# Two late slots of an expert network brought to their nodes by a matrix product instead of by memory

## The reference

```python
scores = x @ Wg + bg
topk_vals, topk_idx = jax.lax.top_k(scores, K)      # K = 2 of 8 experts
gates = jax.nn.softmax(topk_vals, axis=-1)
...
for e in range(NE):
    h = _gelu(x @ W1[e] + b1[e])
    h = _gelu(h @ W2[e] + b2[e])
    y = h @ W3[e] + b3[e]
    out = out + comb[..., e:e + 1] * y
```

## Time and profile before

| | us |
|---|---|
| median of three runs | 2332.95 |
| the runs | 2332.95, 10635.34, 2326.77 |
| the profiled execution, its own time | 2339.89 |
| its span in the profile | 2338.1 |
| network 0, first slot's output to last | 1233.8 to 1362.1 |
| network 1, first slot's output to last | 1981.7 to 2311.6 |

### The profile page before, as it was taken

How to read it: one execution, slowest core, us unless ns; L and a number is a source line. 1 busy time by engine, 2 the same in 40 slices (tenths; PEclk the granted TensorE clock), 3 DMA queues, 4 the chain that set the end, 5 groups by cost and what they waited for, 6 DMA issues and landing times. The chain is left out here.

```text
span 2338.1 us, 32237 instructions
## 1 busy us (share of the span) xinstructions
PE 2099.8 (90%) x12766; PEld 2018.1 (86%) x12766; DVE 1426.8 (61%) x2283; ACT 922.3 (39%) x1220; POOL 393.7 (17%) x216
## 2 busy tenths in 40 slices
PE   6998999999999999999869949788889968999994
PEld 5888999998999999999849949687789947999994
DVE  7645555555763233333459864358984777888884
ACT  2343155555341111111127723125522225777771
POOL 1672400000301434343010022210000020000001
PEclk9999999999999999999969979999999968999997
DMA  6212233333330211110159951110122047999995
GB/s 220 42 29 83 81 116 116 118 133 119 131 139 30 64 41 41 61 41 21 53 196 335 324 197 61 48 45 28 64 65 85 1 154 276 377 375 367 376 365 172
DMA packets 158240, 326.89 MB, mean 140 GB/s; under 512 B 14377, under 2 KB 99337, under 8 KB 158091
## 3 DMA queue, kind: packets, MB, share of 16 engines
q1 hardware_dynamic: 133354, 265.66, 32.5%
q10 hardware_dynamic: 18976, 43.31, 5.3%
q0 software_dynamic: 5760, 15.86, 2.2%
HBM read 278.22 MB, written 46.49 MB: 139 GB/s over the span
## 5 line engine op out<-in xcount | busy, mean ns | idle before, releaser
L656 PE MATMUL banks<-weight_hi,xt_hi 128*128 128x384 f32 (+2 forms) x2208 | 738.9, 335 | 45.3 <-DVE xt_lo L1432 14.3
L659 PE MATMUL banks<-weight_lo,xt_hi 128*128 128x384 f32 (+2 forms) x2208 | 723.5, 328 | 0.0
L660 PE MATMUL banks<-weight_hi,xt_lo 128*128 128x384 f32 (+2 forms) x2208 | 722.8, 327 | 0.0
L656 PEld LDWEIGHTS banks<-weight_hi,xt_hi 128*128 128x128 f32 x2208 | 423.3, 192 | 57.0 <-issue 28.2
L659 PEld LDWEIGHTS banks<-weight_lo,xt_hi 128*128 128x128 f32 x2208 | 423.4, 192 | 0.4 <-issue 0.2
L660 PEld LDWEIGHTS banks<-weight_hi,xt_lo 128*128 128x128 f32 x2208 | 422.5, 191 | 0.0
L1897 DVE TENSOR_TENSOR weight_lo<-weight_raw,weight_hi 128x2304 fp32r<-128x2304 f32 (+2 forms) x153 | 340.9, 2242 | 57.6 <-ACT weight_hi L1160 57.1
L1160 ACT ACTIVATE weight_hi<-weight_raw 128x2304 fp32r<-128x2304 f32 (+2 forms) x153 | 286.7, 1883 | 100.9 <-DMA weight_raw<-L_ffn_w_in 44.1
L859 POOL TENSOR_TENSOR weight_hi<-weight_raw,columns 128x2304 fp32r<-128x2304 f32 x20 | 80.6, 4029 | 700.3 <-DMA weight_raw<-L_gnn_root_in 322.6
L1660 DVE TENSOR_TENSOR held_lo<-banks,held_hi 128x384 fp32r<-128x384 f32 x80 | 44.6, 558 | 213.0 <-ACT held_hi L1087 213.0
L2517 PE MATMUL banks<-held_hi,a_rel 128*128 128x384 f32 (+1 forms) x550 | 170.6, 338 | 3.6 <-ACT a_rel L1102 2.8
(11 more groups left out here) (404 smaller groups left out, 3486.9 us busy)
## 6 DMA issues: line engine op xcount, KB each, us to landing
weight_raw<-L_ffn_w_in SPq DMA_DIRECT2D x102, 1152.0 KB, 7.7
weight_raw<-L_gnn_W_in SPq DMA_DIRECT2D x32, 1152.0 KB
weight_raw<-L_ffn_W_in SPq DMA_DIRECT2D x17, 1152.0 KB, 9.9
products<-bias_rows SPq DMA_DIRECT2D x80, 192.0 KB, 1.9
slot_in<-slot_rows ACTq DMA_DIRECT2D x34, 384.0 KB, 5.6
slot_out<-bias_rows ACTq DMA_DIRECT2D x34, 384.0 KB, 7.2
weight_raw<-L_ffn_W_in SPq DMA_DIRECT2D x17, 576.0 KB, 9.0
product_back<-products SPq DMA_DIRECT2D x10, 960.0 KB, 4.7
```

What stands on the lines that cost most here:

```text
L656: ins = pe.matmul(dst, s[0], m[0], start=start, stop=False)
L659: pe.matmul(dst, s[0], m[1], start=False, stop=False)
L660: return pe.matmul(dst, s[1], m[0], start=False, stop=stop)
```

## The change

The outputs of slots 15 and 16 (`LATE = 2`) no longer go to memory. Instead:

- `slot_out` ends at slot 14. POOL's ten gathers wait for the stores up to slot 14 only, and read row `min(place, 1919)`. They land in buffers that are free by then (the slot inputs, `y_rows`, and the two further raw buffers; from tile 2 on POOL also waits until the last weight unit has left those). The gate of a choice whose row lies in slot 15 or 16 is set to zero for them.
- ACT's queue writes the rows' numbers (before the first turn) and the gates (turn 3) to memory, 128 by 10 floats each, and at turn 5 reads them back broadcast to all partitions (two DMAs of 128 by 1280 floats).
- At turn 8 DVE runs `late_rows`: it finds for each row of slots 15 and 16 its gate, and builds a 0/1 matrix of each slot (128 rows by 640 nodes) in columns of `XT` that the network does not use.
- The outputs of slots 15 and 16 are multiplied by the rows' gates, split into high and low part (ACT, then DVE) and kept in `XT`. For each tile TensorE multiplies them with the 0/1 matrices (`late_products`, 8 matmuls), and DVE adds the result to `X` (`late_sums`).
- The sums with the gathered rows are moved ahead of the last slot's output on DVE: all five tiles in network 1, tiles 0 and 1 in network 0 (tile 2 follows that output; tiles 3 and 4 are added in the mixer's loop).
- The first Q unit's load is issued and its parts are split before the last slot's output; the second one's parts are split inside the mixer's loop.

Four semaphores of the routing are merged into others, which moves no work. The diff, without those:

```diff
@@ -84,6 +84,11 @@
...
+LATE = 2
+LATE_FROM = XSLOTS - LATE
+LATE_ROW = LATE_FROM * SLOT_ROWS
+PLACES = TILES * CHOSEN * P // 4
@@ -582,7 +592,21 @@
...
-        out_rows = [[V, XN1], [x[:, :, :].rearrange("p k c -> p (k c)").bitcast(F32).rearrange("p (t d) -> p t d", t=TILES) for x in XT]]
...
+        choice_all = [x[:, 0:4, 2 * P:2 * P + PLACES] for x in XT_place]
+        late_row, late_gate = first_at[:, 0:LATE], is_more[:, 0:LATE]
+        place_main = others[:, :, :].rearrange("p t e -> p (t e)")[:, 0:CHOICES].bitcast(I32)
...
+
+        def late_cols(s, t):
+
+            return XT[s][:, 4 + t // 3, free.start + t % 3 * P:free.start + (t % 3 + 1) * P]
+
+        out_rows = [x[:, :] for x in slot_in] + y_rows + [r[:, i * DIM:(i + 1) * DIM] for r in raw_more for i in range(3)]
+        LAST_RAW = [max(u for u in range(SPLITS[n]) if UNIT_AT[n][u][0] >= 2) for n in range(2)]
+        LAST_RAW0 = max(u for u in range(SPLITS[0]) if UNIT_AT[0][u][0] == 0)
+        LATE_BANKS = [[0, 4, 6, 4, 6], [0, 5, 3, 0, 5]]
@@ -830,10 +854,12 @@
...
-            sp.wait_ge(e_lo[0], RAWS + SPLITS[0])
+            sp.wait_ge(e_lo[0], RAWS + LAST_RAW0 + 1)
...
             with sp.Fori(0, 3) as i:
                 for c in range(2):
+                    if c == 1:
+                        sp.wait_ge(e_lo[0], RAWS + SPLITS[0])
                     load(Unit(U_MIX1 + c, i, 2), chunks(a["L1_mix_w_qkv"])[:, :, ds((2 * i + c) * WCOL, WCOL)])
@@ -923,20 +949,25 @@
...
                 for b in range(2):
-                    pool.wait_ge(y_out[n][b], 16 * len(range(b, XSLOTS, 2)))
+                    pool.wait_ge(y_out[n][b], 16 * len(range(b, LATE_FROM, 2)))
+                pool.wait_ge(placed, 3 * (n + 1))
                 for t in range(TILES):
+                    if t == 2:
+                        pool.wait_ge(e_lo[n], RAWS + LAST_RAW[n] + 1)
                     for k in range(CHOSEN):
                         j = t * CHOSEN + k
-                        pool.indirect_dma_start(out=out_rows[n][k][:, t, :], out_offset=None, in_=slot_out_dram[n],
-                                                in_offset=bass.IndirectOffsetOnAxis(ap=place[:, j:j + 1], axis=0)).then_inc(back[t], 16)
+                        pool.indirect_dma_start(out=out_rows[j], out_offset=None, in_=slot_out_dram[n],
+                                                in_offset=bass.IndirectOffsetOnAxis(ap=place_main[:, j:j + 1], axis=0)).then_inc(back[t], 16)
 
             after_phase(pool, 2)
             expert_rows(0)
@@ -1183,6 +1214,13 @@
...
+                    if v >= LATE_FROM:
+                        s = v - LATE_FROM
+                        act.wait_ge(late_hot, TILES * LATE * (n + 1))
+                        for c, (bank, _, width) in enumerate(full_cols(n, last)):
+                            act.wait_ge(y_full[n], 2 * v + c + 1)
+                            act.activation(late_y[s][0][:, c, :], ps[:, bank, 0:width], ACT.Copy, scale=late_gate[:, s:s + 1]).then_inc(late_hi, 1)
+                        return
                     act.wait_ge(y_used[n], 2 * (v + 1))
                     act.dma_start(slot_at(slot_out_dram[n], v), y_rows[v % 2]).then_inc(y_out[n][v % 2], 16)
 
@@ -1193,7 +1231,16 @@
...
+                act.wait_ge(placed, 3 * n + 2)
+                act.dma_start(choice_dram[0], place_f[:, :]).then_inc(choice_moved, 16)
                 for turn in turns(n):
+                    if turn == 3:
+                        act.wait_ge(comb_ready, 2 * (n + 1))
+                        act.dma_start(choice_dram[1], gate[:, :, :].rearrange("p t k -> p (t k)")).then_inc(choice_moved, 16)
+                    if turn == 5:
+                        act.wait_ge(choice_moved, 64 * n + 32)
+                        for into, src in zip(choice_all, choice_dram):
+                            act.dma_start(into, src.rearrange("p j -> (p j)").partition_broadcast(P).rearrange("p (c n) -> p c n", c=4)).then_inc(choice_moved, 16)
                     for l, v in visits(n, turn):
                         if l > 0:
                             transposed_hi(l, v)
@@ -1210,11 +1257,11 @@
...
+                    act.wait_ge(e_used[0], LAST_RAW0 + 1)
+                    unit_hi(U_MIX1)
+                    act.activation(warm[:, LN_IN1:LN_IN1 + 1], eps_col[:, :], ACT.Sqrt)
                 rows_out(XSLOTS - 1)
-                if n == 0:
-                    act.wait_ge(e_used[0], SPLITS[0])
-                    for c in range(2):
-                        unit_hi(U_MIX1 + c)
 
             experts(0, a["L0_ffn_Wg"], a["L0_ffn_bg"], a["L0_ffn_b3"], [a["L0_ffn_b1"], a["L0_ffn_b2"]])
             end_phase(act, "act", 3)
@@ -1908,11 +1957,43 @@
...
-                    if v >= 2:
+                    if 2 <= v < LATE_FROM:
...
                     for c, (bank, cols, width) in enumerate(full_cols(n, last)):
+                        if v >= LATE_FROM:
+                            s = v - LATE_FROM
+                            hi, lo = at(late_y[s], slice(None), c)
+                            vec.wait_ge(late_hi, 2 * (LATE * n + s) + c + 1)
+                            vec.scalar_tensor_tensor(lo, ps[:, bank, 0:width], late_gate[:, s:s + 1], f32(hi), ALU.mult, ALU.subtract).then_inc(y_used[n], 1)
+                            continue
                         vec.wait_ge(y_full[n], 2 * v + c + 1)
...
+                def late_rows():
+
+                    vec.wait_ge(masks, 2 + 4 * (n + 1))
+                    vec.tensor_scalar(place_main, place_f[:, :], float(LATE_ROW - 1), None, ALU.min).then_inc(placed, 1)
+                    vec.wait_ge(choice_moved, 64 * n + 32)
+                    flat = gate[:, :, :].rearrange("p t k -> p (t k)")
+                    order.step(vec.scalar_tensor_tensor(flat, place_f[:, :], float(LATE_ROW), flat, ALU.is_lt, ALU.mult))
+                    vec.wait_ge(choice_moved, 64 * (n + 1))
+                    at_all = choice_all[0].rearrange("p c (n t k) -> p t k c n", t=TILES, k=CHOSEN)
+                    for s in range(LATE):
+                        sums = late_gate[:, s:s + 1], total[:, s:s + 1]
+                        for i in range(2):
+                            one_slot = slice(2 * i, 2 * i + 2)
+                            order.step(vec.scalar_tensor_tensor(choice_kept, choice_all[0][:, one_slot], late_row[:, s:s + 1], choice_all[1][:, one_slot],
+                                                                ALU.is_equal, ALU.mult, accum_out=sums[i]))
+                            order.wait()
+                        order.step(vec.tensor_tensor(sums[0], sums[0], sums[1], ALU.add))
+                        order.wait()
+                    for s in range(LATE):
+                        into = [late_cols(s, t).rearrange("p (c n) -> p c n", c=4) for t in range(TILES)]
+                        for t in range(TILES):
+                            order.step(vec.tensor_scalar(into[t], at_all[:, t, 0], late_row[:, s:s + 1], None, ALU.is_equal))
+                        order.wait()
+                        for t in range(TILES):
+                            vec.scalar_tensor_tensor(into[t], at_all[:, t, 1], late_row[:, s:s + 1], f32(into[t]), ALU.is_equal, ALU.add).then_inc(late_hot, 1)
 
                 for _ in range(FIRST[n]):
                     low()
@@ -1921,6 +2002,8 @@
...
+                    if turn == 8:
+                        late_rows()
@@ -1936,23 +2019,28 @@
...
+                if n == 0:
+                    unit_lo(U_MIX1)
+                for t in range(TILES if n == 1 else 2):
+                    expert_sums(n, t)
                 output(XSLOTS - 1)
-
                 if n == 0:
-                    for c in range(2):
-                        unit_lo(U_MIX1 + c)
+                    expert_sums(0, 2)
...
 
                 rows = slice(0, LAST if t == FULL else P)
                 vec.wait_ge(back[t], 16 * CHOSEN * (n + 1))
                 for k in range(CHOSEN):
-                    ins = vec.scalar_tensor_tensor(X[rows, t, :], out_rows[n][k][rows, t, :], gate[rows, t, k:k + 1], X[rows, t, :], ALU.mult, ALU.add)
-                    if n == 0 or k == 0:
-                        order.step(ins)
-                        order.wait()
-                    else:
-                        ins.then_inc(rows_done, 1)
+                    order.step(vec.scalar_tensor_tensor(X[rows, t, :], out_rows[t * CHOSEN + k][rows, :], gate[rows, t, k:k + 1], X[rows, t, :], ALU.mult, ALU.add))
+                    order.wait()
+
+            def late_sums(n, t):
+
+                rows, bank = slice(0, LAST if t == FULL else P), LATE_BANKS[n][t]
+                x_row = X[rows, t, :].rearrange("p (c n) -> p c n", c=2)
+                vec.wait_ge(y_full[n], 2 * XSLOTS + t + 1)
+                vec.tensor_tensor(x_row, ps[rows, bank:bank + 2, 0:WCOL], x_row, ALU.add).then_inc(y_used[n], 1)
 
             experts(0)
             end_phase(vec, "vec", 3)
@@ -1962,7 +2050,12 @@
...
-                expert_sums(0, t)
```

(30 more changed lines are left out.)

55 lines of the change are left out of this document (34 added, 21 removed).

## The result

The changed kernel takes **2355.82 us** in the median of 4 runs (2348.79 to 2363.86) against 2332.55 for the kernel before, run beside it: 1.0106 [1.0083, 1.0130], 24.7 us more (one run of the kernel before at 10635 us is left out of the ratio). The forecast was 2334.5 and the range ended at 2348: **the prediction was wrong**, by 21 us, although the tail of network 1, at which the change aims, came out as forecast.

A forecast was written before the change was run, and what follows sets the result against it. Bounds: TensorE, DVE and memory near their limits in network 1, loads late in network 0, a serial 27.1 us tail. Terms -14.5 + 2 + 6 + 1 + 5 + 2 = +1.5 us, by the median 2334.5; range 2320 to 2348.

The forecast's parts named there:

- Tail of network 1, -14.5: End of network 1: late products and additions replace the serial gathers and sums after the last expert matmul, -14.5 us.
- I take full clock: Network 1's tail: TensorE's 40 late matmuls run at full clock; half clock would cost 7 us more.
- Gathers, +2: End of network 1: three of ten gathers slowed beside DVE's weight parts, last output slips, +2 us (0 to +5).
- Rival two: DVE's queue ahead of the last slot's output, both networks: every gather slowed and holding it back, +15.5 us, 2348.5; chance 0.15.
- the rule that the prediction named: Gathers beside DVE's two-SBUF-input operations would not be held up, making the gathers' term 0; the prediction went against it.
- Turn 8 of network 1, +6: Build of 9 us ahead of slot 7's output, 3.0 us free, the rest a TensorE stall: +6 us (0 to +9).
- its broadcast, +1: Network 1: two broadcast DMAs of 1.31 MB, 3.5 us, with weights 3 us ahead: +1 us (0 to +3.5).
- Network 0's turns, +5: Network 0: build stalls TensorE 8.5 us in turn 8, 4 won back, broadcast 3.5 us: +5 us (+1 to +12).
- The end of network 0, +2: End of network 0: five additions and a weight part added, six sums moved ahead, a DVE wait: +2 us (-3 to +6).
- The rival that the builds are absorbed: Turn 8 of both networks: build time vanishes in idle DVE time over three or four turns, -8.5 us, 2324.5; chance 0.27.

The follow-up runs named there:

- E4: The changed kernel with network 0 as before, so only network 1 late; ratio to the kernel before 1.0008.
- E3: The kernel before with network 1's broadcast at turn 5 and build in turn 8, results unused; ratio 1.0042.
- E6: The kernel before with broadcast and build (late_rows) in network 0 alone, no late path; ratio 1.0037, 8.7 us.
- E17: The changed kernel with network 1 as before, plus 175 TensorE drains ahead of network 1's first turn; ratio to the kernel before 1.0081.
- E16: The kernel before with 81 idle TensorE drains ahead of network 1's first turn; ratio 1.0040, 9.3 us.
- E18: E11 with 175 TensorE drains ahead of network 1's first turn; ratio to the kernel before 0.9990.
- E11: Changed kernel, network 1 as E8; network 0's build in pieces (turns 9 to 12, 15), its last output ahead of the first sums; ratio to kernel before 1.0014.
- E10: The changed kernel with network 1 as before, so only network 0 late; ratio to the kernel before 1.0125.
- E12: The changed kernel run again, unaltered, beside other versions; ratio to the kernel before 1.0104.
- E8: Changed kernel with network 0 as before, network 1's broadcast ahead of turn 0, build in 14 pieces at ends of turns 4 to 14; ratio to kernel before 0.9957.

## Why the prediction was wrong

**Tail of network 1, -14.5.** Right in mechanism, -12.3 in size. The measured number holds the gathers' slip too, for which the forecast had +2, so -12.3 stands against -12.5; two errors cancel in this, which is luck. The additions stand 1.39 us apart as forecast. TensorE idled 1.86 us ahead of its first late product, in a turn that it had begun after 7.56 us of waiting, and from 2344.57 to 2347.75 its products ran at 0.32 us each instead of 0.17, at a granted clock of 0.50, the lower of the two levels, which the prediction had excluded ("I take full clock"). Ten or so of them make 1.6 us of the 2.2 between -14.5 and -12.3; the gathers make the other 0.6.

**Gathers, +2.** The slowing came as forecast, its cost was smaller: with 1.3 us of waits the sums ended 0.6 us behind the last expert matmul, not 2. In E4's trace waits of 5.3 us put them 6.4 us behind. Rival two, gathers holding the last slot, so did not happen in the changed kernel, but it did in E4. The row won over the rule that the prediction named. The Trainium skill (SBUF — State Buffer, "Who interferes with whom") infers that the writing of descriptors is not hindered by an operation of VectorE with two SBUF inputs. But the two gathers that began beside such a weight part took 2.86 and 2.42 us, ending 0.8 us after it, and the one behind the second took 0.96. The same section also says that such an operation contends with a GpSimd instruction that reads SBUF, and a gather reads its row numbers (`others`) there; the prediction left this half out.

**Turn 8 of network 1, +6, and its broadcast, +1.** Mis-sized. The build takes 10.4 us, not 9: the twenty 128 by 128 instructions take 0.26 and 0.36 each where 0.22 was taken from another form, and each sum of 640 has a read of its accumulator. The 3 us of lead were no longer there in the changed kernel: the broadcast had used them up. Together 9.8 us [6.1, 13.8] by E3 instead of 7. What TensorE waited for in network 1 was the weight part behind the output, not the output itself as foreseen.

**Network 0's turns, +5.** Measured 8.7 [4.4, 12.9] by E6. The broadcast's two parts land in 9.2 and 14.1 us and hold ACT for 2.55, 2.75 and 2.43 us in turns 5 and 6; I had costed it as its bytes, 3.5 us, and had seen no stall of its own. Then the stall of turn 8 comes. Afterwards 60.8 - 57.3 = 3.5 us are won back (forecast 4).

**The end of network 0, +2.** Mis-sized. From slot 14's output to network 1's first one the late path takes 638.8 us where it took 632.0 (E6: 632.1), +6.8; the seven traces with this end have 635.6 to 640.4, the ten with the old one 631 to 634. By ratios E17 less E6 gives 10.2, on different chips. The transposes came 1.6 us later than before where the forecast had them 0.6 earlier: three tiles' sums and the slot's output stand ahead of the meeting of the engines, with 1.00 and 1.99 us of waits for gathers, and TensorE's first product came 11.49 us after its last work. By tile 4's last pass it is +4.5 (forecast +1.6): DVE waits for tile 3's product, as foreseen, and for ACT's high part of tile 4. The last 2 us are in the mixer and were not traced to a wait.

**The missing term.** The prediction costs TensorE's and DVE's instructions where they stand and nowhere else. The late path's 81 TensorE instructions in network 0 (40 matmuls, their 40 weight loads and one more) also move every instruction fetch of network 1 by 8 us in its turn, and with weights that only just keep up this is worth 9.3 us [6.3, 12.4] (E16), of which the trace shows 6, and 5.6 where network 1 is late too (E18 less E11, on different chips).

**The sum.** Measured parts: network 0 late 18.9 (E17), network 1 late 1.9 (E4), the fetch 5.6: 26.4 us against 24.7 [19.4, 30.3] measured. That these meet is in part luck: with E16's 9.3 for the fetch they make 30.1. On one chip, E10 has network 0 late with the fetch at 29.3 us and E12 less E10 leaves -4.9 for network 1, within the noise of both. The forecast had 7 for network 0, -5.5 for network 1 and nothing for the fetch.

So two steps failed. The sum for network 0 was 7 and measured 19: its broadcast was costed by bytes and stalled ACT, its build was half won back on paper, and its end was given +2 where the traces show +6.8. And the instruction fetch was a term put at nothing, by leaving it out. The rival that the builds are absorbed has nothing for it in this form, but E8 shows that in pieces they are.

## What to carry to other kernels

Work put in front of an output that the bounding engine waits for costs its full time less the lead, and another part of the same change may eat that lead first: cut it into pieces that fit each turn's idle time, as E8 did. A reordering at the end of a stage is worth what the next stage's first instruction gains, so follow that one through each in-order queue. And where a loop's transfers barely keep pace, check where instruction packets fall before believing a difference under 0.5%. A stretch of one engine shows where it runs late and not yet where the bounding engine loses time. A control with idle instructions in place of the new ones tells a change's work from its place in memory.

## What was not expected of the hardware

- One 16 KB instruction packet in each turn of 21 us (1.67 MB in 102 packets) is worth 0.4% of the run by when it comes: 81 drains in an idle stretch, 1.0040 [1.0027, 1.0053]; weights then land in 8.2 us in the median instead of 7.7. How it does so is open.
- A gather on GpSimd that begins beside a VectorE operation of two SBUF inputs (128x2304, 2.56 us) ends 0.82 to 0.85 us after it: 2.86 and 2.42 us at the end of network 1 and 2.31 at the end of network 0, where 0.96 is usual.
- A broadcast of 640 KB to 128 partitions beside the weights lands in 9.2 us, the second behind it in 14.1 (network 0 of the changed kernel), and the two weight loads of 1152 KB issued in the same 25 us take 14.9, where the three ahead of them took 8.9.
